# Context scores as split fp32r products in a one-core decoder layer, with the second batch's chain moved up in the tensor engine's queue

## The chip, the cores and the metric

The kernel runs on one core of one Trainium2 chip. The metric is the device time of one execution in microseconds; less is better. The profiled execution is one run of its own, so its time and its span are given apart from the median.

## The reference

One decoder layer: self-attention with a causal mask, attention over a context without projections, and a mixture of 16 experts with the best 4 per token, each behind a layer norm and added to its input. Two batches of 256 tokens, width 256, 16 heads of 16, 512 context tokens per batch.

```
x = x + attention(layernorm(x), Wq, bq, Wk, bk, Wv, bv, Wo, bo)      # 16 heads, causal

h = layernorm(x)
scores = einsum('bsd,bmd->bsm', h, ctx) / sqrt(256)
scores = where(mask[:, None, :], scores, -1e30)
x = x + (softmax(scores) @ ctx, or 0 for a batch whose mask is all false)

h = layernorm(x)
logits = h @ router_weight.T + router_bias
w = softmax of the 4 largest logits, at their experts, else 0
x = x + sum_e w[:, e] * (((clip(up_e, -7, 7) + 1) * glu(min(gate_e, 7))) @ down_e + down_bias_e)
```

## The kernel before

Five engines run one instruction stream each, written out by hand in the order in which each engine executes it. A semaphore count stands wherever one engine needs another's result. Nothing reorders the streams, so the place of a call in a block is its place in the queue.

**Tiles.** Tokens lie in four chunks of 128 (0 and 1 are batch 0, 2 and 3 are batch 1). `PS` is the accumulator memory, eight banks of 512 columns. `XH` and `XL` are the high and low part of the transposed activations in fp32r: an fp32 product is made there from three fp32r products (high by high, low by high, high by low). The experts have always been computed like that (`first_gate_up`, L1085, for expert 0, L1119 for the others, L1135 for the down projection). `WHg`, `WLg` are the split weights: the scalar engine writes the high part (L352), GpSimd the low part (L296).

**Self-attention.** A loop over `v` from 0 to 17, two steps a head group. In each the tensor engine does scores (L933, L937), transposes of the probabilities (L947) and, in odd steps, the product with V (L961). The vector engine adds the causal mask and takes the row maximum in one instruction (L668), the scalar engine exponentiates (L382), and both copy the transposed probabilities back (L693, L414). Batch 0 is done by step 10; its output projection and residual fill the later steps.

**Context attention.** For chunk `c`: `context_scores` (L984, fp32 product with `ctxT`, two matmuls, and a third that adds the mask penalty `pen` of one partition through `ones_bf`), `context_max` (L636) and `context_exp` (L386), `context_turn` (L992), `context_take` (L394), `context_values` (L998), `context_out` (L649). Chunks 0 and 1 begin when the loop ends. The second batch's self-attention output is turned back (L969), divided (L609, L610), turned again (L874), projected (L978) and added (L616) among them; then it is centred, turned and copied to `xT`, and chunks 2 and 3 follow. `rstds` (L282) on GpSimd takes the inverse roots for each of the norms.

**Router and first expert.** The last norm is turned and copied to `xT` (L435, L440), from there copied to `XH` (L445), and the rest goes to `XL` (L736). The router's logits are fp32 products with `xT` (`logits_of`, L1010). Some 17 small vector instructions (L750 to L773) choose the experts. `first_gate_up` does expert 0 batch by batch. `keep_warm` (L883) puts unneeded bf16 products in gaps.

**Mask.** The mask is loaded into one partition, cast (L589), and in step 5 made into `pen` and into the flag of a batch with any valid token (L683, L684), which one small matmul (L1033) spreads over the partitions.

Of the kernel before, what the change touches and what calls it, by code (L numbers as in the profile page):

```python
# [6 lines left out]
F32 = mybir.dt.float32  # L7
# [7 lines left out]
P = 128  # L15
B, S, D = 2, 256, 256
M = 512
# [25 lines left out]
def decoder_layer(nc, x_d, ctx_d, ctxT_d, wqkv_d, wo_d, params_d, rows_d, mask_d, dbias_d, we_d, out_d):  # L43
    ctx = ExitStack()
    with ctx:
# [9 lines left out]
        x = sb("x", [P, NC, D])  # L55
        ctx_sb = sb("ctx_sb", [P, B * KM, D])
        ctxT = sb("ctxT", [P, B * KD, M])
        wqkv = sb("wqkv", [P, 3, KD, D])
# [3 lines left out]
        mask8 = sb("mask8", [1, B * M], U8)  # L62
# [13 lines left out]
        ones_bf = sb("ones_bf", [1, P], BF16)  # L76
# [3 lines left out]
        one1 = sb("one1", [1, P])  # L80
# [23 lines left out]
        maskf = sb("maskf", [1, B * M])  # L104
        pen = sb("pen", [1, B * M], BF16)
        valid1 = sb("valid1", [1, B])
        valid = sb("valid", [P, B])
        xmax = sb("xmax", [P, NC])
# [42 lines left out]
        xpt = [keys_flat[:, (2 + i) * M:(3 + i) * M].rearrange("p (c q) -> p c q", q=P) for i in range(2)]  # L151

# [23 lines left out]
        pen_done, valid_ps, valid_done = sem("pen_done"), sem("valid_ps"), sem("valid_done")  # L176
# [70 lines left out]
        def _(pool):  # L247
# [24 lines left out]
            g.memset(ones_bf[:, :], 1.0)  # L272
            g.memset(ones_f[:, :], 1.0)
            g.memset(one1[:, :], 1.0)
# [35 lines left out]

            low_keys(0)
# [3 lines left out]
            low_gate_up(1, 1)  # L315
            for n in range(1, 5):
                rstds(n)
# [17 lines left out]
        def _(act):  # L335
# [5 lines left out]
            act.dma_start(mask8[:, :], mask_d.rearrange("(a n) -> a n", a=1)).then_inc(mask_in, 16)  # L341
# [44 lines left out]
            def context_exp(c):  # L386

                act.wait_ge(xbias_done, c + 1)
                if c >= 2:
                    act.wait_ge(xpT_done, c - 1)  # L390
                a.activation(xp[c % 2], PS[:, XS_BANK[c], :], ACT.Exp, bias=xbias[:, c:c + 1], scale=xscale[:, c:c + 1],
                             accum_out=xsum[:, c:c + 1]).then_inc(xexp_done, 1)

            def context_take(c):  # L394
                act.wait_ge(xpT_done, c + 1)
                if c >= 2:
                    act.wait_ge(xav_done, c - 1)
                a.activation(xpt[c % 2].rearrange("p h q -> p (h q)"), PS[:, XT_BANK[c], :], ACT.Copy
                             ).then_inc(xpt_done, 1)

            for v in range(NV + 2):
# [20 lines left out]
                if v == NV:  # L422
                    context_exp(0)
# [5 lines left out]
            context_take(0)  # L429
            context_exp(1)  # L430

            def take_turned(dst, b, bank, n, done):

                act.wait_ge(lnT_done, n)
                a.activation(dst[:, :, b * S:(b + 1) * S], PS[:, bank, :].rearrange("p (k n) -> p k n", k=KD), ACT.Copy  # L435
                             ).then_inc(done, 1)
# [6 lines left out]
            def high_x(b, count, tokens):  # L443
                act.wait_ge(xT_done[b], count)
                a.activation(XH[:, :, tokens], xT[:, :, tokens], ACT.Copy).then_inc(xh_done, 1)  # L445

            take_chunk(attT, 2, 7, 5, attT_done[1])
            context_take(1)
            take_chunk(attT, 3, 3, 6, attT_done[1])
            take_chunk(xT, 2, 7, 7, xT_done[1])  # L450
            take_chunk(xT, 3, 3, 8, xT_done[1])
            context_exp(2)
            take_turned(xT, 0, 0, 9, xT_done[0])
            context_exp(3)
            context_take(2)
            high_x(0, 3, slice(0, S))
            context_take(3)
            take_chunk(xT, 2, 6, 10, xT_done[1])
            high_x(1, 4, slice(S, S + P))
            take_chunk(xT, 3, 4, 11, xT_done[1])  # L460
            high_x(1, 5, slice(S + P, T))
# [65 lines left out]
        def _(dve):  # L527
# [61 lines left out]
            link(v_.tensor_copy(maskf[:, :], mask8[:, :]))  # L589
# [68 lines left out]

            for v in range(NV + 2):
# [13 lines left out]
                if v == NV:  # L673
                    dve.wait_ge(lnT_done, 4)
# [35 lines left out]
                if v >= NV:  # L710
                    context_max(v - NV)
# [502 lines left out]
```

## Time and profile before

| | us |
|---|---|
| median of 3 runs | 232.87 (232.74 to 234.01) |
| the profiled execution's own time | 232.66 |
| its span | 230.9 |
| around the span | 1.76 |

| engine | busy us | share of the span |
|---|---|---|
| tensor, matmuls | 222.6 | 96% |
| tensor, weight loads | 177.8 | 77% |
| vector | 179.4 | 78% |
| scalar | 130.1 | 56% |
| GpSimd | 75.2 | 33% |

A matmul's end is modelled, so the step from one start to the next tells what it costs, and its own duration tells only when its result can be used. The clock granted to the tensor engine is full in all 40 slices of the page. From 91.2 us on the program is the loop over experts; what the change touches lies before that.

### The profile page before, as it was taken

Reading aid. Unit: us, or ns where it says so; the run is one execution under the profiler, and the core shown is the slowest. Engines: PE = TensorE matmul, PEld = TensorE weight load, DVE = VectorE, ACT = ScalarE, POOL = GpSimd, SP = SyncE. Lnnn points to the kernel's source line nnn. Section 1 sums busy time; section 2 is a strip of 40 time slices with the busy share of each in tenths; the row PEclk is TensorE's granted clock in tenths of the full one; section 3 lists DMA queues with packets and bytes.
Section 4 is the critical chain, followed back from the end, with each engine's and each line's share of the span. In section 5 each row is a group of like instructions: output and inputs, shape, how many; then the busy total and the mean of one; then the engine's idle time right before and its main releaser. Section 6 shows DMA issues by size and latency. Waiting matters only on the chain.

```text
span 230.9 us, 4563 instructions
## 1 busy us (share of the span) xinstructions
PE 222.6 (96%) x1481; PEld 177.8 (77%) x1481; DVE 179.4 (78%) x431; ACT 130.1 (56%) x258; POOL 75.2 (33%) x65
## 2 busy tenths in 40 slices
PE   7999989998999999989999999999999999999995
PEld 2588767875485788778888888888888888888884
DVE  3779896969267458679889879879879879879775
ACT  2138999766341617384484384385385385375561
POOL 6621460001002010426426426425425435435222
PEclk9999999999999999999999999999999999999999
DMA  5991042000000000022422431331331330410002
GB/s 170 381 387 34 0 140 91 3 4 0 0 3 0 0 0 4 0 62 76 139 60 77 136 71 65 136 79 57 136 88 48 136 102 34 136 45 0 1 3 91
DMA packets 7856, 17.30 MB, mean 75 GB/s; under 512 B 913, under 2 KB 2978, under 8 KB 7714
## 3 DMA queue, kind: packets, MB, share of 16 engines
q1 hardware_dynamic: 7232, 16.52, 21.8%
q10 hardware_dynamic: 610, 0.60, 0.9%
q8 instruction: 8, 0.13, 0.2%
q14 instruction: 6, 0.05, 0.1%
HBM read 16.59 MB, written 0.52 MB: 74 GB/s over the span
## 4 chain that ended last, share of the span: by engine, by line
PE 79%; DVE 9%; ACT 6%; issue 3%; POOL 2%; POOLq 0%; DVEq 0%; ACTq 0%
PE PS L1119 34%; PE PS L1135 20%; PE PS L987 3%; ACT pr L382 3%; PE PS L1001 3%; PE PS L1085 3%; DVE masked L668 2%; PE PS L947 2%; PE PS L961 2%; PE PS L978 2%; PE PS L895 2%; PE PS L883 1%; DVE HL L798 1%; PE PS L1165 1%; DVE qpar L574 1%
## 5 line engine op out<-in xcount | busy, mean ns | idle before, releaser
L296 POOL TENSOR_TENSOR WLg<-raw_g,WHg 128x1024 fp32r<-128x1024 f32 x16 | 38.2, 2390 | 58.4 <-ACT WHg L352 58.4
L793 DVE SCALAR_TENSOR_TENSOR pt<-pt 128x512 f32<-128x512 f32 x30 | 49.4, 1646 | 4.2 <-DVE pt L789 2.2
L478 ACT ACTIVATE HH<-pt 128x512 fp32r<-128x512 f32 x30 | 18.9, 632 | 52.3 <-DVE pt L793 52.1
L1119 PE MATMUL PS<-XH,WHg 128*128 128x512 f32 x120 | 47.0, 392 | 0.0
L1119 PE MATMUL PS<-XL,WHg 128*128 128x512 f32 x120 | 46.9, 390 | 0.0
L1119 PE MATMUL PS<-XH,WLg 128*128 128x512 f32 x120 | 46.7, 389 | 0.0
L1135 PE MATMUL PS<-WHd,HH 128*128 128x256 f32 x120 | 35.3, 294 | 1.0 <-DVE HL L798 0.8
L1135 PE MATMUL PS<-WLd,HH 128*128 128x256 f32 x120 | 33.9, 282 | 0.0
L1135 PE MATMUL PS<-WHd,HL 128*128 128x256 f32 x120 | 33.9, 282 | 0.0
L303 POOL TENSOR_TENSOR WLd<-raw_w,WHd 128x512 fp32r<-128x512 f32 x16 | 20.7, 1296 | 32.9 <-ACT WHd L358 32.9
L798 DVE TENSOR_TENSOR HL<-pt,HH 128x512 fp32r<-128x512 f32 x30 | 22.2, 738 | 11.0 <-ACT HH L478 11.0
L382 ACT ACTIVATE pr<-masked,nmax 128x128 f32<-128x128 f32 x64 | 23.7, 443 | 7.2 <-DVE nmax L668 7.2
L1135 PEld LDWEIGHTS PS<-WHd,HH 128*128 128x128 f32 x120 | 22.9, 190 | 6.4 <-issue 4.8
L1119 PEld LDWEIGHTS PS<-XH,WLg 128*128 128x128 f32 x120 | 22.5, 188 | 4.8
L1119 PEld LDWEIGHTS PS<-XH,WHg 128*128 128x128 f32 x120 | 22.6, 188 | 4.5 <-issue 0.2
L1119 PEld LDWEIGHTS PS<-XL,WHg 128*128 128x128 f32 x120 | 22.6, 188 | 4.1
L782 DVE SCALAR_TENSOR_TENSOR x<-PS,score,x 128x256 f32<-128x256 f32 x56 | 24.2, 473 | 0.0
L1135 PEld LDWEIGHTS PS<-WHd,HL 128*128 128x128 f32 x120 | 22.9, 191 | 0.0
L1135 PEld LDWEIGHTS PS<-WLd,HH 128*128 128x128 f32 x120 | 22.9, 191 | 0.0
L668 DVE CUSTOM_DVE_ANT_0 masked<-PS,causal 128x128 f32<-128x128 f32 x64 | 18.9, 350 | 3.3 <-PE PS L937 3.2
L472 ACT ACTIVATE pt<-PS,bup 128x512 f32<-128x512 f32 x30 | 20.6, 686 | 0.0
L469 ACT ACTIVATE pt<-PS,params 128x512 f32<-128x512 f32 x30 | 20.4, 679 | 0.0
(154 smaller groups left out, 358.5 us busy)
## 6 DMA issues: line engine op xcount, KB each, us to landing
raw_g<-we_d SPq DMA_DIRECT2D x16, 512.0 KB, 4.0
raw_w<-we_d SPq DMA_DIRECT2D x16, 256.0 KB, 2.6
ctxT<-ctxT_d SPq DMA_DIRECT2D x1, 1024.0 KB, 10.1
ctx_sb<-ctx_d SPq DMA_DIRECT2D x1, 1024.0 KB, 12.3
wqkv<-wqkv_d SPq DMA_DIRECT2D x3, 256.0 KB, 6.1
out_d<-x SPq DMA_DIRECT2D x4, 128.0 KB, 1.7
rows<-rows_d ACTq DMA_DIRECT2D x1, 264.0 KB, 5.7
x<-x_d ACTq DMA_DIRECT2D x2, 128.0 KB, 2.8
```

The source lines that it names most:

```text
L296: g.tensor_tensor(WLg[slot][:, :, :, :].rearrange("p k g f -> p (k g f)"), raw_g[slot][:, :], WHg[slot][:, :, :, :].rearrange("p k g f -> ...
L303: g.tensor_tensor(WLd[slot][:, :, :].rearrange("p k d -> p (k d)"), raw_w[slot][:, :], WHd[slot][:, :, :].rearrange("p k d -> p (k d)").bi ...
L382: i = a.activation(pr[:, v % 2, j, cols], masked[:, v % 2, j, cols], ACT.Exp, bias=nmax[:, v % 2, j, qc:qc + 1], scale=-1.0)
L469: a.activation(glu[:, m, :], PS[:, 2 * m, :], ACT.Gelu_apprx_sigmoid, bias=gub[:, bass.ds(e, 1), 0, m]).then_inc(glu_done, 1)
L472: a.activation(upc[:, m, :], PS[:, 2 * m + 1, :], ACT.Identity, bias=bup1[:, bass.ds(e, 1), m]).then_inc(up_done, 1)
L478: a.activation(HH[slot][:, m, :], hid[:, m, :], ACT.Copy).then_inc(hh_done, 1)
L668: i = v_.tensor_tensor_reduce(out=masked[:, v % 2, j, cols], in0=PS[:, 2 * (v % 3) + j, cols], in1=causal[:, cols], scale=1.0, scalar=HUGE ...
L782: v_.scalar_tensor_tensor(out=acc[:, c, :], in0=PS[:, 4 + 2 * slot + c // 2, (c % 2) * D:(c % 2 + 1) * D], scalar=score[:, c, bass.ds(e, 1 ...
L793: v_.scalar_tensor_tensor(out=hid[:, m, :], in0=glu[:, m, :], scalar=GLU_MAX, in1=upc[:, m, :], op0=ALU.min, op1=ALU.mult).then_inc(hid_do ...
L798: v_.tensor_tensor(HL[slot][:, m, :], hid[:, m, :], HH[slot][:, m, :].bitcast(F32), ALU.subtract).then_inc(hl_done, 1)
L1119: i = t.matmul(PS[:, 2 * m + part, :], w[slot][:, k, part, m * P:(m + 1) * P], xx[:, k, :], start=(n == 0), stop=(n == 3 * KD - 1))
L1135: i = t.matmul(PS[:, 4 + 2 * slot + c // 2, (c % 2) * D:(c % 2 + 1) * D], hh[slot][:, k, c * P:(c + 1) * P], w[slot][:, k, :], start=(n == ...
```

## The change

- `ctxT` is split into `keys_high0`, `keys_high1` and `keys_low` by four GpSimd instructions on 128x1024 (`split_keys`), the router's weights into `rth`, `rtl` (`split_router`). The new tiles lie over `x`, `ctxT` and `wqkv`.
- `context_scores` is six fp32r matmuls of 512 columns per chunk instead of two fp32 ones and one for the mask. `logits_of` is six fp32r matmuls of 16 columns per chunk instead of two fp32 ones.
- The mask is loaded into all 128 partitions. The vector engine reduces it to `valid`; GpSimd casts it and makes `pen` of it (`masks`). The matmul L1033 is gone. `context_max` adds `pen` and takes the maximum in one instruction whose sums go to SBUF (`xp`), and `context_exp` reads them there.
- The turned activations go from `PS` into `XH` (scalar engine) and as difference into `XL` (vector engine) without `xT` between.
- In the queues of all engines the second batch's turning back, turning and projection stand ahead of the context products of the first, the two halves of batch 0's `first_gate_up` stand around the last turn, batch 1's logits behind it, and the four `keep_warm` calls there are gone.

```diff
-        mask8 = sb("mask8", [1, B * M], U8)
+        mask8 = sb("mask8", [P, B * M], U8)
...
+            def masks():
...
+                pool.wait_ge(mask_in, 16)
+                linked(g.tensor_copy(pen[:, :], mask8[:, :]))
+                pool.wait_ge(valid_done, 1)
+                for b in range(B):
+                    g.tensor_scalar(pen[:, b * M:(b + 1) * M], pen[:, b * M:(b + 1) * M], valid[:, b:b + 1], -NEG,
+                                    ALU.subtract, ALU.mult).then_inc(pen_done, 1)
+            def split_router():
+                pool.wait_ge(param_in, 16)
+                g.tensor_copy(rth[:, :, :], routerT).then_inc(router_high, 1)
+                pool.wait_ge(router_high, 1)
+                g.tensor_tensor(rtl[:, :, :], routerT, rth[:, :, :].bitcast(F32), ALU.subtract).then_inc(router_low, 1)
+            def split_keys(b):
+                pool.wait_ge(ctxT_in, 16)
+                if b == 1:
+                    pool.wait_ge(v_ps, NC)
+                raw = ctxT[:, b * KD:(b + 1) * KD, :]
+                g.tensor_copy(cth[b], raw).then_inc(cth_done, 1)
+                pool.wait_ge(cth_done, b + 1)
+                g.tensor_tensor(ctl[b], raw, cth[b].bitcast(F32), ALU.subtract).then_inc(ctl_done, 1)
...
             low_gate_up(1, 1)
+            masks()
+            split_router()
+            split_keys(0)
+            split_keys(1)
             for n in range(1, 5):
                 rstds(n)
...
-                if v == NV:
-                    context_exp(0)
+                if v == NV - 1:
+                    high_tokens(7, 4, slice(0, S), yh_done)
...
-            link(v_.tensor_copy(maskf[:, :], mask8[:, :]))
+            v_.tensor_reduce(valid[:, :], mask8[:, :].rearrange("p (b m) -> p b m", b=B), AX.X, ALU.max).then_inc(valid_done, 1)
...
-                link(v_.tensor_reduce(xmax[:, c:c + 1], PS[:, XS_BANK[c], :], AX.X, ALU.max))
+                link(v_.tensor_tensor_reduce(out=xp[c % 2], in0=PS[:, XS_BANK[c], :], in1=pen[:, c // QC * M:(c // QC + 1) * M],
+                                             scale=1.0, scalar=-HUGE, op0=ALU.add, op1=ALU.max, accum_out=xmax[:, c:c + 1]))
...
                 if v == NV:
-                    dve.wait_ge(lnT_done, 4)
-                    v_.tensor_copy(xT[:, :, 0:S], PS[:, 7, :].rearrange("p (k n) -> p k n", k=KD)).then_inc(xT_done[0], 1)
+                    low_tokens(7, yh_done, 1, slice(0, S), yl_done)
...
-            normalise(x3, 3, (0, 1))
             context_max(2)
             context_max(3)
+            normalise(x3, 3, (0, 1))
...
-                pe.wait_ge(xT_done[b], 2 if b == 0 else c - QC + 2)
+                pe.wait_ge(yl_done, 1 if b == 0 else c)
+                pe.wait_ge(ctl_done, b + 1)
...
-                t.matmul(PS[:, XS_BANK[c], :], ones_bf[:, :], pen[:, b * M:(b + 1) * M], start=False, stop=True
-                         ).then_inc(xs_done, 1)
+                    for xx, w in ((XH, cth), (XL, cth), (XH, ctl)):
+                        i = t.matmul(PS[:, XS_BANK[c], :], xx[:, k, c * P:(c + 1) * P], w[b][:, k, :],
+                                     start=(n == 0), stop=(n == 3 * KD - 1))
```

The tensor engine's queue behind the self-attention loop, before: context scores, turning back (L969), context values, turns of `att` (L874), projection (L978).

```order
L987 MATMUL PS<-ctxT,xT 128x512 x2
L988 MATMUL PS<-pen,ones_bf 128x512
L995 MATMUL PS<-ident,qpar 128x128 x4
L969 MATMUL PS<-ident,osum 128x128 x8
L1001 MATMUL PS<-ctx_sb,qpar 128x256 x4
L874 MATMUL PS<-ident,att 128x128 x2
L995 MATMUL PS<-ident,qpar 128x128 x4
L874 MATMUL PS<-ident,att 128x128 x2
L978 MATMUL PS<-wo,attT 128x256 x4
L1001 MATMUL PS<-ctx_sb,qpar 128x256 x4
```

The same place after (L1039 is the context turn, L1009 the turning back, L1045 the context values, L1018 the projection).

```order
L1030 MATMUL PS<-keys_low,XH 128x512
L1009 MATMUL PS<-ident,osum 128x128 x8
L1039 MATMUL PS<-ident,qpar 128x128 x4
L914 MATMUL PS<-ident,att 128x128 x4
L1018 MATMUL PS<-wo,attT 128x256 x4
L1045 MATMUL PS<-ctx_sb,qpar 128x256 x4
L1039 MATMUL PS<-ident,qpar 128x128 x4
L914 MATMUL PS<-ident,xn 128x128 x4
L1045 MATMUL PS<-ctx_sb,qpar 128x256 x4
L1030 MATMUL PS<-keys_high,XH 128x512
```

The projection no longer stands behind `context_values(0)` and `context_turn(1)`, and `context_values(1)` has moved behind the turns of batch 1's centred rows, straight ahead of its scores.

The scalar engine's queue at the end of the self-attention loop, before.

```order
L414 ACTIVATE pt<-PS 128x384
L421 ACTIVATE osum<-PS 128x256
L414 ACTIVATE pt<-PS 128x384
L391 ACTIVATE qpar,xsum<-PS,xbias,xscale 128x512
L421 ACTIVATE osum<-PS 128x256
```

The same place after.

```order
L463 ACTIVATE pt<-PS 128x384
L470 ACTIVATE osum<-PS 128x256
L448 ACTIVATE XH<-PS 128x2x256
L463 ACTIVATE pt<-PS 128x384
L470 ACTIVATE osum<-PS 128x256
L430 ACTIVATE qpar,xsum<-qpar,xbias,xscale 128x512
```

The high part of batch 0's turned rows is a new step of this queue, behind the copies of step 15; in front of the scores stood one copy on the vector engine before.

GpSimd's queue between the attention's weight splits and the second `rstds`, after; before, nothing stood between the rows L302 and L288.

```order
L302 TENSOR_TENSOR WLg<-raw_g,WHg 128x1024
L325 CAST pen<-mask 128x1024
L328 TENSOR_SCALAR pen<-pen,valid 128x512 x2
L334 CAST rth<-params 128x32
L336 TENSOR_TENSOR rtl<-params,rth 128x32
L344 CAST keys_high<-ctxT 128x1024
L346 TENSOR_TENSOR keys_low<-ctxT,keys_high 128x1024
L344 CAST keys_high<-ctxT 128x1024
L346 TENSOR_TENSOR keys_low<-ctxT,keys_high 128x1024
L288 TENSOR_TENSOR rstd<-ve,half 128x2 x4
```

## Rows read from the trace of the kernel before

**Rows 1.** Stretch by engine: length, busy (instructions) PE, PEld, DVE, ACT, POOL, clock, DMA

```profile
57.69:91.22 33.53, 33.06 (x196) 23.54 (x195) 19.23 (x72) 12.66 (x29) 2.12 (x3) 1.00 0.00 0
100.13:217.00 116.87, 116.64 (x659) 99.90 (x660) 100.07 (x142) 68.95 (x111) 48.98 (x27) 1.00 0.26 83
```

**Rows 2.** Timeline of the tensor engine, context attention: start, us, instruction

```profile
57.69 1.96 PE L987 MATMUL PS<-ctxT,xT 128*128 128x512 f32 x4
...
59.89 0.86 PE L961 MATMUL PS<-pt,vp 128*32 128x128 f32 x24
...
63.40 1.04 PE L969 MATMUL PS<-ident,osum 128*128 128x128 f32 x8
...
67.02 2.04 PE L978 MATMUL PS<-wo,attT 128*128 128x256 f32 x8
...
71.91 1.98 PE L987 MATMUL PS<-ctxT,xT 128*128 128x512 f32 x4
...
76.87 0.60 PE L995 MATMUL PS<-ident,qpar 128*128 128x128 f32 x4
...
79.10 3.62 PE L1001 MATMUL PS<-ctx_sb,qpar 128*128 128x256 f32 x16
```

**Rows 3.** Timelines of the scalar and vector engine around the scores and splits

```profile
57.88 0.49 ACT L414 ACTIVATE pt<-PS 128x384 f32<-128x384 f32 x1
...
77.07 0.60 ACT L435 ACTIVATE xT<-PS 128x512 f32<-128x512 f32 x1 [0.63 <-PE PS L867]
...
79.53 0.69 DVE L736 TENSOR_TENSOR XL<-xT,XH 128x512 fp32r<-128x512 f32 x1 [0.65 <-ACT XH L445]
```

**Rows 4.** Chain that ended last: fp32r products of 256 and of 512 columns

```profile
82.72 2.86 PE PS L1085 x24
...
91.22 3.01 PE PS L1119 x12
```

**Rows 5.** Timeline of the tensor engine, the router's logits of one chunk

```profile
86.38 0.62 PE L1010 MATMUL PS<-params,xT 128*128 128x16 f32 x4
86.85 0.38 PE L883 MATMUL PS<-warm 128*128 128x512 bf16 x1
```

**Rows 6.** Timeline of the vector engine: row maximum, last norm, routing

```profile
74.60 0.68 DVE L639 TENSOR_REDUCE xmax<-PS 128x1 f32<-128x512 f32 x1
...
85.00 0.73 DVE L553 TENSOR_SCALAR xn<-x,mv,rstd 128x256 f32<-128x256 f32 x2 [0.81 <-POOL rstd L282]
...
87.87 0.21 DVE L750 TENSOR_TENSOR logits<-PS,rows 128x64 f32<-128x64 f32 x1
```

**Rows 7.** Timeline of GpSimd: fill, weight splits, inverse roots

```profile
3.93 0.94 POOL L276 MEMSET vp<- 128x1024 f32 x1
...
29.41 1.39 POOL L303 TENSOR_TENSOR WLd<-raw_w,WHd 128x512 fp32r<-128x512 f32 x1 [0.58 <-ACT WHd L358]
32.38 2.37 POOL L296 TENSOR_TENSOR WLg<-raw_g,WHg 128x1024 fp32r<-128x1024 f32 x1 [1.58 <-ACT WHg L352]
54.72 0.75 POOL L282 TENSOR_TENSOR rstd<-ve,half 128x2 f32<-128x2 f32 x1 [19.97 <-DVE ve L626]
```

**Rows 8.** Timeline of the vector engine around the mask, at the start and in step 5

```profile
10.35 0.67 DVE L589 CAST maskf<-mask 1x1024 f32<-1x1024 uint8 x1
...
12.61 1.53 DVE L574 TENSOR_SCALAR qpar<-PS,params,parity 128x512 f32<-128x512 f32 x2 [0.81 <-PE PS L895]
...
29.58 1.20 DVE L684 TENSOR_REDUCE valid<-maskf 1x2 f32<-1x1024 f32 x1
```

**Rows 9.** Timelines from the routing to expert 0's down projection, engine by engine

```profile
90.39 0.69 ACT L469 ACTIVATE pt<-PS,params 128x512 f32<-128x512 f32 x1
...
94.61 2.40 POOL L296 TENSOR_TENSOR WLg<-raw_g,WHg 128x1024 fp32r<-128x1024 f32 x1 [9.64 <-ACT WHg L352]
...
95.31 2.24 DVE L798 TENSOR_TENSOR HL<-pt,HH 128x512 fp32r<-128x512 f32 x1
...
100.13 0.39 PE L1135 MATMUL PS<-WHd,HH 128*128 128x256 f32 x1 [0.81 <-DVE HL L798]
```

More of the change, by code:

```diff
@@ L399, in context_take, with turned, high_tokens @@
                              ).then_inc(xpt_done, 1)
+            def turned(bank, tokens):
+                n = tokens.stop - tokens.start
+                return PS[:, bank, 0:KD * n].rearrange("p (k n) -> p k n", k=KD)
+            def high_tokens(bank, n, tokens, done):
+                act.wait_ge(lnT_done, n)
+                a.activation(XH[:, :, tokens], turned(bank, tokens), ACT.Copy).then_inc(done, 1)
             for v in range(NV + 2):
@@ L428, in _ @@
                     high_gate_up(1, 1, 0)
[L429 to L436, printed above, removed]
+            context_exp(0)
             def take_chunk(dst, c, bank, n, done):
@@ L657, in context_stats, with low_tokens @@
                 row_stats(x3, c)
+            def low_tokens(bank, high, n, tokens, done):
+                dve.wait_ge(high, n)
+                count = tokens.stop - tokens.start
+                v_.tensor_tensor(XL[:, :, tokens], PS[:, bank, 0:KD * count].rearrange("p (k n) -> p k n", k=KD),
+                                 XH[:, :, tokens].bitcast(F32), ALU.subtract).then_inc(done, 1)
             for v in range(NV + 2):
@@ L709, in _ @@
                     centre(0)
-                if v >= NV:
-                    context_max(v - NV)
+                if v == NV + 1:
+                    dve.wait_ge(pen_done, B)
+                    context_max(0)
             for qc in range(QC):
                 outputs(1, qc, (5, 0)[qc])
-            dve.wait_ge(valid_done, 1)
+            context_max(1)
             context_weight(0)
-            context_weight(1)
-            context_out(0)
-            for j in range(QC):
-                residual(1, j, PS[:, (6, 5)[j], 0:D])
+            residual(1, 0, PS[:, 6, 0:D])
+            residual(1, 1, PS[:, 5, 0:D])
             centre(1)
             context_scale(1)
+            context_out(0)
+            context_weight(1)
+            low_tokens(7, yh_done, 2, slice(S, S + P), yl_done)
+            low_tokens(3, yh_done, 3, slice(S + P, T), yl_done)
             context_out(1)
@@ L1003, in context_values, with logits_of @@
                 i.then_inc(xav_done, 1)
-            def logits_of(b, count, chunks):
-                pe.wait_ge(xT_done[b], count)
+            def logits_of(count, chunks):
+                pe.wait_ge(router_low, 1)
+                pe.wait_ge(xl_done, count)
                 for c in chunks:
+                    n = 0
                     for k in range(KD):
-                        i = t.matmul(PS[:, 7, c * E:(c + 1) * E], xT[:, k, c * P:(c + 1) * P], routerT[:, k, :],
-                                     start=(k == 0), stop=(k == KD - 1))
+                        for xx, w in ((XH, rth), (XL, rth), (XH, rtl)):
+                            i = t.matmul(PS[:, 7, c * E:(c + 1) * E], xx[:, k, c * P:(c + 1) * P], w[:, k, :],
+                                         start=(n == 0), stop=(n == 3 * KD - 1))
+                            n += 1
                 i.then_inc(logit_ps, 1)
@@ L1094, in _ @@
                 turn_chunk(xn, QC + j, (6, 4)[j])
[L1095 to L1100 removed]
+            first_gate_up(0, 1)
+            logits_of(2, (2,))
+            logits_of(3, (3,))
+            first_gate_up(1, 0)
+            first_gate_up(1, 1)
             def turn_scores():
```

142 lines of the change are left out of this document (65 added, 77 removed).

## The prediction, made before the changed kernel was run

> **What bounds the kernel now.** I read the busy time by stretch first. Between the first context scores at 57.69 us and expert 1 at 91.22 the tensor engine is busy 33.06 of 33.53 us, and from 100.13 to 217 it is busy 116.64 of 116.87 [rows 1]. So behind 100.13 the end moves by as much as the product at 100.13 moves, and that is the date to follow. Next come the waits. The product at 100.13 waited 0.81 us for the vector engine's `HL` [rows 9]. The first `HL` of expert 0, at 95.31, lasted 2.24 us [rows 9], where the `XL` of the same shape lasts 0.69 [rows 3]; GpSimd's `WLg` ran from 94.61 to 97.01 [rows 9], and `HL` ended half a microsecond behind it. That `WLg` hangs, through the scalar engine's copies and the first product of expert 0, on the routing, whose first instruction stands at 87.87 [rows 6]. So two dates count: when the router's logits are there, and when the tensor engine gets to expert 1.
>
> The Trainium skill (SBUF — State Buffer, "Who interferes with whom") says that a vector instruction with two SBUF inputs and a GpSimd instruction that reads SBUF exclude each other for a whole instruction. By that rule the 2.24 us are a wait for `WLg`, and the trace agrees.
>
> **The scores.** Before, one chunk's scores took the tensor engine 2.20 us (57.69 to 59.89, [rows 2]). After, it is six fp32r products of 512 columns. Twelve such took 3.01 us with the tail of the last [rows 4], some 0.235 each, so six take 1.4. That saves 0.8 a chunk, 3.2 us of tensor time in four. I do not take that as the gain, because each place has a wait of its own, so I walk the queues with these durations.
>
> **First scores.** Before, they stood ready behind the last attention turn, at 57.69. After, the scalar engine must write `XH`, and its queue is free for that at 57.88, where the next copy of step 15 began. The copy takes 0.60 and the difference 0.69 [rows 3], with two handovers of some 0.05. The scores start at about 59.25, 1.55 later, and end at 60.65, 0.75 later. Behind this wait stand, on the tensor engine, the last product with V and, on the vector engine, the copy of the last probabilities that this product needs; both come within the 0.75. The second scores win 0.8 back: the tensor engine is level with before at about 62.85.
>
> **Second batch's chain.** The turning back (8 transposes, 1.04 us, [rows 2]) comes ahead of one context turn (4 transposes, so 0.5): 0.5 earlier. The projection stood at 67.02, behind one chunk's context values (two chunks take 3.62, [rows 2]; I take 1.75 a chunk) and another context turn. Both now come behind it. It starts at 65.1, as soon as the two `att` chunks are divided, turned and copied, and is 1.9 earlier; so are batch 1's centred rows. But `context_values(1)` now stands between them and the scores of chunk 2, which begin at 71.8 against 71.91 [rows 2]. Two scores take 2.8 for 4.4: 1.7 won at their end.
>
> **Maxima.** Adding the mask inside the maximum costs little: the old maximum takes 0.68 [rows 6], the new one has the same 512 columns and a read of the result behind it. I take 0.77. But the vector engine reaches chunk 2 only behind `context_out(1)`, statistics and variances, at 73.6; the old one stood at 74.60 [rows 6]. With exponent and handovers the context turn of chunk 2 starts at 75.6 against 76.87 [rows 2]: 1.25 won. Two turns, the transposes and two times 1.75 of values bring the end of the values to 81.2, 1.35 earlier. The last norm hangs on it and comes at 83.65 against 85.00 [rows 6].
>
> **Router and expert 0.** Here the win is spent. The fp32 logits of a chunk take 0.47 for four passes of 16 columns, 0.117 each (86.38 to 86.85, [rows 5]), as long as a product of 256 columns (24 in 2.86, 0.119, [rows 4]): something other than the columns bounds them. The same pitch for fp32r makes 12 products 1.4 us (0.91 before) and each six 0.69 (0.47 before). The tensor engine goes on almost without a gap: logits of batch 0 to 82.6, half of expert 0 (12 products, 1.43) to 84.05, two turns to 84.6, the other half to 86.05, six logits to 86.75, six to 87.45. The splits of the last rows (scalar from 84.3, vector to 85.8) hide behind the second half. The last product is usable 0.2 later, and the same walk on the kernel before comes out 0.15 early, so the routing starts at 87.8 against 87.87 [rows 6]: 0.1 won of 1.35. The half of `first_gate_up` ahead of the last logits, and 0.9 us of extra logits, ate it. Batch 1's 24 products end at 90.5.
>
> **To the loop.** Expert 1 started at 91.22 [rows 4]. It needs the tensor engine (90.5) and a bank that the scalar engine has emptied, at 91.08 before [rows 9], which hangs on the routing: 0.1 earlier. `WLg` and the blocked `HL` hang on the same routing: the product at 100.13 comes 0.1 earlier, with a longer wait before it.
>
> **GpSimd.** The new work starts where the last `WLg` ends, at 34.75 (32.38 plus 2.37, [rows 7]). No row shows a cast there. From above: five instructions of 1024 at 2.37, two of 512 at 1.39, two small at 0.75, 16.1 us, to 50.9. From below: three of 1024 at the fill's 0.94, two at 2.37, two of 512 at 0.47, 8.5 us, to 43.3 [rows 7]. It is needed at 54.72 by the `rstd` behind it [rows 7] and later by the scores. I take it as hidden, 3.8 us clear even at the upper end. The attention's vector instructions in that stretch read `PS` and at most one SBUF tile, unlike the blocked `HL`, so I charge no contention. If that cover were gone, every microsecond past 54.72 would count whole.
>
> The Trainium skill (GPSIMD Engine Reference, "Engine selection") puts one-input work on GpSimd near line rate. By that the list would end near my lower end; nothing in the sum changes.
>
> **Start.** The mask is 128 KB for 1 KB. The reduction takes 1.20 where the cast took 0.67 at 10.35; the next need is at 12.61, for which the vector engine had waited 0.81 [rows 8]. The 0.53 fits in it. It costs nothing if the mask has landed by 10.6; between 0 and 0.3 us, I take 0. The mask work that leaves step 5 (1.20 of it in [rows 8]) was no gain either: the scalar engine set the pace there.
>
> **Sum.** Start 0, scores and chains -1.35, logits and the half expert +1.25: -0.1 us. The profiled execution of 232.66 would be 232.56; it lies 0.21 under the median of 232.87. Forecast: 232.8.
>
> **Rivals.** A measurement of this kernel can tell about 0.5% from no change, 1.16 us.
> 1. The win reaches the routing. If an fp32r product with 16 columns costs half that pass (the lower bound is the 0.036 of the products with V, 24 in 0.86, [rows 2]), 0.6 more comes early. If then `HL` also slips in ahead of `WLg`, the wait of 0.81 goes: -0.1 -0.6 -0.8 = -1.5, 231.4. For it: what bounds a pass may be less in fp32r. Against it: `WLg` began 0.7 ahead of `HL`, and both move together. Chance of all this, or of as much through a shorter chain of norms, 0.25; of the first half alone (232.2) 0.12.
> 2. GpSimd becomes late. From 20.0 us of new work on (54.72 less 34.75) each further microsecond delays batch 0's scale, the exponents and the chain by one. The inverse root takes 0.75 for two columns [rows 7], so this engine has slow operations, and one with two steps and a scalar from memory is not in the trace. With 22 us: +2.0, 234.9. Chance 0.07.
> 3. The mask lands late, one for one from 10.6 on; at 11.5 +0.9, 233.7. Chance 0.06, half of it beyond the 0.5%.
> 4. The clock. It is full in both stretches [rows 1]. The warming calls go, and gaps of 1.4 and 1 us come in. If it fell to 1.2 GHz for 2.5 us worth of products, +2.5: 235.3. Chance 0.03.
>
> The forecast itself has 0.47; its own spread is 232.2 to 233.3, mostly the pitch of the small products (0.14 for 0.117 gives +0.4). Faster by over 0.5%: 0.25. Within: 0.62. Slower: 0.13. The range reaches down to rival 1, 231.4, and to 233.9, past rival 3.
>
> **What would show it.** Right: the first key product at 59.2; the projection near 65.1; the last context values done near 81.2; logits for the vector engine at 87.8; again a first `HL` of over 2 us; a wait of about a microsecond near 100. Wrong: small products at half the pitch; a first `HL` of 0.69; GpSimd busy at 54; a clock below full.

## The result

The kernel went from 232.74 us (median of 5 runs, 232.55 to 234.01) to 230.81 (median of 5, 230.67 to 232.31), a ratio of 0.9924 with a 95% interval of 0.9896 to 0.9952. That is 1.9 us faster, outside the predicted range, where the forecast had said 232.8 and no measurable change.

In some executions, of every kernel here, TensorE is granted half its clock in some stretch, and the mean granted clock of the run reads 0.99 in place of 1.00. The kernel before takes 232.5 to 232.9 us with and without it in most executions (a few lie between 233.1 and 233.8), and 233.9 to 234.2 where the mean reads 0.985. The changed kernel takes 230.7 to 231.0 without it (231.4 once) and 232.2 to 232.7 with it. A few runs are longer still, such as two of ten of the changed kernel, run again, at 235.2 and 235.4 with a mean of 0.98, and no ratio here uses them. The profiled execution of the changed kernel (232.31, span 230.2) is one with a stretch of half clock.

Two stretches of that execution follow, in the columns of [rows 1]. The first is the first context scores; the second is as long as the second line of [rows 1] and starts at the same product:

```profile
59.84:62.30 2.46, 2.46 (x6) 1.81 (x6) 0.41 (x1) 0.00 (x0) 0.00 (x0) 0.50 0.00 0
...
101.93:218.80 116.87, 116.81 (x671) 102.91 (x672) 97.52 (x144) 72.53 (x114) 55.73 (x28) 1.00 0.26 83
```

The second line is what the prediction did not expect. The tensor engine is as busy as before, 116.81 of 116.87 us, and yet 671 matmuls are recorded where [rows 1] had 659 in the same time. Its busy share had hidden a wait. The product that the prediction followed came later, not earlier: 101.93 against 100.13 [rows 9]. From it to the end of the span it was 130.8 us before (230.9 less 100.13) and is 128.3 now (230.2 less 101.93). So the change lost 1.8 us ahead of the loop over the experts in this execution, and the loop, whose code did not change, gave back 2.5.

Where the 1.8 went is in the timelines of the changed kernel (start, us, instruction, in brackets the idle time before it and what ended it): the vector engine at the start, the tensor engine's first attention score and first context score, its projection, and then GpSimd, the vector and the tensor engine around expert 0:

```profile
11.61 1.22 DVE L628 TENSOR_REDUCE valid<-mask 128x2 f32<-128x1024 uint8 x1 [1.56 <-DMA mask<-mask_d]
...
16.56 0.45 PE L973 MATMUL PS<-kT,qpar 32*128 32x128 f32 x3 [0.72 <-DVE HL L619]
...
59.84 0.79 PE L1030 MATMUL PS<-keys_high,XH 128*128 128x512 f32 x1 [1.30 <-DVE XL L705]
60.43 0.63 PE L1030 MATMUL PS<-keys_high,XL 128*128 128x512 f32 x1
60.85 0.63 PE L1030 MATMUL PS<-keys_low,XH 128*128 128x512 f32 x1
...
67.30 1.99 PE L1018 MATMUL PS<-wo,attT 128*128 128x256 f32 x8
...
96.41 2.40 POOL L302 TENSOR_TENSOR WLg<-raw_g,WHg 128x1024 fp32r<-128x1024 f32 x1 [10.72 <-ACT WHg L393]
...
97.12 2.24 DVE L838 TENSOR_TENSOR HL<-pt,HH 128x512 fp32r<-128x512 f32 x1
...
101.93 0.38 PE L1174 MATMUL PS<-WHd,HH 128*128 128x256 f32 x1 [0.81 <-DVE HL L838]
```

The mask landed at about 11.6, and with it the first attention score moved from 15.96 to 16.56 (the work behind it by 0.7). The six context products, at half clock in this execution, come every 0.43 us in place of the 0.235 of [rows 4]: 1.2 us. The rest, 1.8 less 0.7 less 1.2, is -0.1, which is what the prediction had for the whole context stage.

One kernel of the experiments (`after_dve_pause`, the changed kernel with one tiny instruction more) was profiled with a mean clock of 0.999, and there the changed stage can be read without any half clock. Its first attention score is at 16.55 us, 0.6 later than before. Then come the last norm, the routing and the product that the prediction followed:

```profile
84.39 0.73 DVE L593 TENSOR_SCALAR xn<-x,mv,rstd 128x256 f32<-128x256 f32 x2 [0.81 <-POOL rstd L289]
...
88.33 0.22 DVE L791 TENSOR_TENSOR logits<-PS,rows 128x64 f32<-128x64 f32 x1 [1.77 <-PE PS L1060]
...
100.60 0.39 PE L1177 MATMUL PS<-WHd,HH 128*128 128x256 f32 x1 [0.81 <-DVE HL L841]
```

So with a full clock the product comes 0.5 us later than the 100.13 of [rows 9]: 0.6 from the start, -0.1 from the context stage.

### The profile page after: what moved, and what is told of

It is laid out like the page before. It is cut to its first block, busy times and chain, and to the rows that moved or that the text cites. A ratio compares the mean times of both kernels' runs of the same rounds, so it can differ in the third digit from the quotient of the medians.

```text
span 230.2 us, 4585 instructions
## 1 busy us (share of the span) xinstructions
PE 217.4 (94%) x1484; PEld 181.1 (79%) x1485; DVE 173.5 (75%) x434; ACT 131.2 (57%) x256; POOL 92.3 (40%) x72
## 4 chain that ended last, share of the span: by engine, by line
PE 74%; DVE 10%; ACT 6%; DMA 4%; issue 3%; ACTq 1%; DVEq 0%
PE PS L1158 35%; PE PS L1174 19%; DMA mask<-mask_d 4%; PE PS L1030 3%; PE PS L1045 3%; ACT pr L423 3%; DVE masked L717 2%; PE PS L987 2%; PE PS L1001 2%; PE PS L1018 2%; PE PS L1125 1%; PE PS L1204 1%; DVE HL L838 1%; PE PS L973 1%; PE PS L1057 1%
## 5 line engine op out<-in xcount | busy, mean ns | idle before, releaser
L302 POOL TENSOR_TENSOR WLg<-raw_g,WHg 128x1024 fp32r<-128x1024 f32 x16 | 41.2, 2574 | 61.0 <-ACT WHg L393 61.0
L838 DVE TENSOR_TENSOR HL<-pt,HH 128x512 fp32r<-128x512 f32 x30 | 30.7, 1025 | 12.2 <-ACT HH L517 12.2
L833 DVE SCALAR_TENSOR_TENSOR pt<-pt 128x512 f32<-128x512 f32 x30 | 36.2, 1206 | 4.2 <-DVE pt L829 1.8
L1174 PE MATMUL PS<-WHd,HH 128*128 128x256 f32 x120 | 34.2, 285 | 0.9 <-DVE HL L838 0.8
L309 POOL TENSOR_TENSOR WLd<-raw_w,WHd 128x512 fp32r<-128x512 f32 x16 | 23.4, 1463 | 22.0 <-ACT WHd L399 22.0
## 6 DMA issues: line engine op xcount, KB each, us to landing
ctxT<-ctxT_d SPq DMA_DIRECT2D x1, 1024.0 KB, 11.6
```

The source lines that it names most:

```text
L302: g.tensor_tensor(WLg[slot][:, :, :, :].rearrange("p k g f -> p (k g f)"), raw_g[slot][:, :], WHg[slot][:, :, :, :].rearrange("p k g f -> ...
L309: g.tensor_tensor(WLd[slot][:, :, :].rearrange("p k d -> p (k d)"), raw_w[slot][:, :], WHd[slot][:, :, :].rearrange("p k d -> p (k d)").bi ...
L833: v_.scalar_tensor_tensor(out=hid[:, m, :], in0=glu[:, m, :], scalar=GLU_MAX, in1=upc[:, m, :], op0=ALU.min, op1=ALU.mult).then_inc(hid_do ...
L838: v_.tensor_tensor(HL[slot][:, m, :], hid[:, m, :], HH[slot][:, m, :].bitcast(F32), ALU.subtract).then_inc(hl_done, 1)
L1174: i = t.matmul(PS[:, 4 + 2 * slot + c // 2, (c % 2) * D:(c % 2 + 1) * D], hh[slot][:, k, c * P:(c + 1) * P], w[slot][:, k, :], start=(n == ...
```

## What happened in the loop

The loop over the experts has two bodies, one for each of two buffers, and a pass does two experts. In the kernel before, GpSimd's `WLg` and the vector engine's second activation product (`pt<-pt`, the step that makes `hid`) start within 0.05 us of each other in every expert of it (0.12 in the one ahead of it), and the one that starts later is held: a race. Both hang on the scalar engine's copy `HH`: the one through the next copy `WHg`, the other through `HL` and the clamp. The kernel before, one such place, engine by engine:

```profile
171.05 0.63 ACT L478 ACTIVATE HH<-pt 128x512 fp32r<-128x512 f32 x1 [0.35 <-DVE pt L793]
171.59 1.05 ACT L352 ACTIVATE WHg<-raw_g 128x1024 fp32r<-128x1024 f32 x1
...
171.72 0.69 DVE L798 TENSOR_TENSOR HL<-pt,HH 128x512 fp32r<-128x512 f32 x1 [0.70 <-ACT HH L478]
172.33 0.42 DVE L789 TENSOR_SCALAR pt<-pt 128x512 f32<-128x512 f32 x1
172.84 2.89 DVE L793 SCALAR_TENSOR_TENSOR pt<-pt 128x512 f32<-128x512 f32 x1
...
172.80 2.39 POOL L296 TENSOR_TENSOR WLg<-raw_g,WHg 128x1024 fp32r<-128x1024 f32 x1 [2.95 <-ACT WHg L352]
```

The same place after, in the second body of the loop:

```profile
172.10 0.69 DVE L833 SCALAR_TENSOR_TENSOR pt<-pt 128x512 f32<-128x512 f32 x1
172.71 0.87 DVE L822 SCALAR_TENSOR_TENSOR x<-PS,score,x 128x256 f32<-128x256 f32 x2
173.50 2.12 DVE L838 TENSOR_TENSOR HL<-pt,HH 128x512 fp32r<-128x512 f32 x1
...
172.14 2.93 POOL L302 TENSOR_TENSOR WLg<-raw_g,WHg 128x1024 fp32r<-128x1024 f32 x1 [3.04 <-ACT WHg L393]
```

Before, `WLg` is 0.04 us ahead, and the product is held until it is done: 2.89 us for work of 0.69. After, the product is 0.04 ahead; now `WLg` is held (2.93 for 2.39) and then `HL` (2.12 for 0.69). The Trainium skill (SBUF — State Buffer, "Who interferes with whom") says that issue order and not the shape of the operation decides who blocks; these two places agree, and they show how narrow the decision is.

It matters who is held, because the second product stands on the ring that feeds the tensor engine (product, `HH`, `WHd`, bank reading, product), and `HL` only on the down projection. The scalar engine's groups between 127 and 210 us, before and then after (count | busy, mean ns | idle before it, and what ended most of it):

```profile
L472 ACT ACTIVATE pt<-PS,bup 128x512 f32<-128x512 f32 x19 | 13.0, 687 | 0.0
L469 ACT ACTIVATE pt<-PS,params 128x512 f32<-128x512 f32 x19 | 12.9, 678 | 0.0
L478 ACT ACTIVATE HH<-pt 128x512 fp32r<-128x512 f32 x19 | 12.0, 632 | 32.2 <-DVE pt L793 32.2
```

```profile
L508 ACT ACTIVATE pt<-PS,params 128x512 f32<-128x512 f32 x21 | 14.3, 680 | 3.5 <-PE PS L1158 3.5
L511 ACT ACTIVATE pt<-PS,bup 128x512 f32<-128x512 f32 x20 | 13.7, 686 | 5.6 <-PE PS L1158 5.2
L517 ACT ACTIVATE HH<-pt 128x512 fp32r<-128x512 f32 x20 | 12.6, 632 | 22.4 <-DVE pt L833 21.4 <-PE PS L1174 0.7
```

Before, the scalar engine never waits for the tensor engine's products: the ring of scalar and vector engine set the pace, and two experts took 17.15 us (`WLg` at 172.80, the next of that body at 189.95). After, it waits 8.7 us for them: two experts take 16.66 (172.14, 188.80) and the tensor engine is the bound. Experiment 1 bears this out: with the short product in both bodies the pace stays at 16.68. In the page the mean of all thirty such products fell from 1646 to 1206 ns and that of `HL` rose from 738 to 1025.

In the changed kernel this begins at the second body's first pass, and there GpSimd starts late:

```profile
114.59 2.40 POOL L302 TENSOR_TENSOR WLg<-raw_g,WHg 128x1024 fp32r<-128x1024 f32 x1 [3.08 <-ACT WHg L393]
118.89 1.30 POOL L309 TENSOR_TENSOR WLd<-raw_w,WHd 128x512 fp32r<-128x512 f32 x1 [1.90 <-ACT WHd L399]
123.50 2.65 POOL L302 TENSOR_TENSOR WLg<-raw_g,WHg 128x1024 fp32r<-128x1024 f32 x1 [3.31 <-ACT WHg L393]
```

From the end of the scalar copy to the start of `WLg` it is 0.17 us at 114.59, 0.53 at 123.50, and 0.25 in every later pass of this body (0.17 still in the first body). The 0.08 between 0.17 and 0.25 is just what flips the order, from `WLg` 0.04 us ahead to the product 0.04 ahead. The experiments ask where this comes from and what it is worth.

## Experiments

Each is named by what it starts from. "Full clock" means the runs with a mean granted clock of 1.00.

**1. Does losing the race cost what the loop lost? `before_pool_pause`.** In the kernel before, a tiny operation ahead of each `WLg` of the loop:

```
+                if not isinstance(e, int):
+                    g.tensor_tensor(pause[:, bass.ds(e, 1), :], half[:, :].unsqueeze(1), half[:, :].unsqueeze(1), ALU.subtract)
                 g.tensor_tensor(WLg...
```

> The kernel before with one small GpSimd instruction (128x4) ahead of each WLg of the loop, so that WLg starts 0.2 to 0.3 us later and the vector engine's second product stands first. Phase theory: that product lasts 0.69 us, WLg is held instead, an expert takes 8.34 us for 8.6, in 11 or 12 experts 2.3 to 3.0 us less: 229.8 to 230.5. Rival (the loop gained through something static of the changed kernel, such as where its tiles or its code lie): the time stays at 232.7 or rises by up to 0.3.

229.61 and 229.71 at full clock, 230.93 to 231.06 at 0.993 and 232.38 at 0.985, beside 232.71: ratio 0.9915 (0.9882 to 0.9948). Both bodies now have the short product:

```profile
162.60 0.69 DVE L796 SCALAR_TENSOR_TENSOR pt<-pt 128x512 f32<-128x512 f32 x1
163.21 0.87 DVE L785 SCALAR_TENSOR_TENSOR x<-PS,score,x 128x256 f32<-128x256 f32 x2
164.00 2.27 DVE L801 TENSOR_TENSOR HL<-pt,HH 128x512 fp32r<-128x512 f32 x1
...
163.31 2.41 POOL L299 TENSOR_TENSOR WLg<-raw_g,WHg 128x1024 fp32r<-128x1024 f32 x1
```

So the order in this race is enough for the loop's gain, and it is worth 3 us to the kernel before, with no part of the change. That kernel is also faster than the changed one. `before_again`, the kernel before unchanged on the same chip, gave 232.63 with the product at 2.9 us in every expert of the loop.

> The kernel before, traced a second time. Phase theory: in the loop over experts GpSimd's WLg again starts 0.03 to 0.05 us ahead of the vector engine's second product in every expert, that product lasts 2.9 us in every expert, and an expert takes 8.6 us. Chance theory (who starts first is drawn anew in each execution): some of the products of 0.69 us, experts of 8.34 us between.

**2. The other way round: `after_dve_pause`.** A fill on the vector engine ahead of the second product, to hand the race back.

```
                     wait(dve, hl_done, e * 2 + (m - 1))
+                    if not isinstance(e, int) and m == 1:
+                        v_.memset(pause[:, :], 0.0)
```

> The changed kernel with one small vector instruction ahead of the second product of each expert of the loop, so that GpSimd's WLg stands first by 0.05 to 0.1 us in every expert. Phase theory: the product lasts 2.9 us in all of them, an expert takes 8.6 us or a little more, and the gain of the loop goes: 2.2 to 3 us more than the changed kernel, 233.0 to 233.8. Rival (static): 230.8 to 231.0.

The expected 233.0 to 233.8 did not come, and the run decides nothing: 230.68 (clock 0.999) and 230.99 (1.00), 231.54 to 232.16 at 0.993. The fill moved the product by only 0.03 us, and in the second body it still went first, in a tie of the records (both at 170.87, product 0.69, `WLg` 2.95). So the race was not handed back; the recorded starts are a little coarser than what decides.

**3. The start: `after_valid_late`.** The mask reduction moves from the start into step 5 of the attention.

```
-            dve.wait_ge(mask_in, 16)
-            v_.tensor_reduce(valid[:, :], mask8[:, :]...)
...
+                if v == 5:
+                    dve.wait_ge(mask_in, 16)
+                    v_.tensor_reduce(valid[:, :], mask8[:, :]...)
```

> The changed kernel with the reduction of the mask moved from the start into step 5 of the self-attention, so that nothing at the start waits for the mask's load. If the late mask cost the start its 0.7 us: 230.1 (230.0 to 230.3), and the first attention scores at 15.9 us for 16.56. Rival (the start was late for another reason, such as the other loads landing about a microsecond later): 230.8, scores as late as now. Either holds only if the loop keeps its 8.34 us.

229.94, 230.06 and 230.25 at full clock against 230.67 to 231.0 of the changed kernel: 0.7 us. In its trace the first attention score stands at 15.71, where the kernel before has 15.96. So the late mask was the whole loss at the start.

**4. Where the loop lies: `before_pool_pad` and `after_pool_pad`.** The change puts nine instructions into GpSimd's stream ahead of the loop and takes two fills out; the loop itself is untouched. Here seven tiny subtractions, where GpSimd is idle:

```
+            for n in range(7):
+                g.tensor_tensor(pad[:, n, :], half[:, :], half[:, :], ALU.subtract)
             for n in range(1, 5):
                 rstds(n)
```

> The kernel before with seven tiny GpSimd subtractions (128x4, about 0.1 us each) put behind its low weight parts and ahead of the expert loop, where GpSimd is idle in both kernels. They take no shared resource at any moment of the loop; all they change is where the loop's instructions lie in GpSimd's stream, by as many instructions as the change adds net. Placement theory: the weight subtraction of the loop's second body then starts about 0.25 us after its ScalarE copy (0.16 before) with one late start near 120 us, the second activation product of those experts takes 0.7 us in place of 2.9, and the time falls by 2.2 to 2.6 us to 230.1 to 230.6. Rival (the changed context stage itself sets the phase of the loop): nothing moves, 232.7, product 2.9 us in every expert.

> The changed kernel with the same seven tiny GpSimd subtractions ahead of its loop, which moves the loop on by seven more instructions. Placement theory: the pattern of long and short second products can move to the other body or vanish; if it vanishes (2.9 us in every expert) the time is 233.0 to 233.4, if it stays 230.7 to 231.0. Rival (the context stage sets it): the pattern and 230.8 stay whatever the placement. A time above 232.5 with products of 2.9 us would show placement alone; 230.8 with the pattern as it was leaves it open.

`before_pool_pad` came out wrong for both theories: 233.52 at full clock, median 233.68, ratio 1.0038 (1.0024 to 1.0052), every second product at 2.9 us. But its trace kept the placement theory alive: the late start is there, but one GpSimd operation further on, on `WLd` of the second body:

```profile
121.73 2.40 POOL L297 TENSOR_TENSOR WLg<-raw_g,WHg 128x1024 fp32r<-128x1024 f32 x1 [2.95 <-ACT WHg L355]
126.38 1.29 POOL L304 TENSOR_TENSOR WLd<-raw_w,WHd 128x512 fp32r<-128x512 f32 x1 [2.25 <-ACT WHd L361]
```

That is 0.51 us behind its copy, later passes 0.25. There it wins no race and costs: two experts take 17.26 us (`WLg` at 148.02 and at 165.28). `after_pool_pad` lost the late start and the pattern altogether: 234.0 in the profiled run, median 235.29, ratio 1.0119 (1.0098 to 1.014), slower than the kernel before and above the 233.4 expected at most.

**5. Put it where the change puts it: `before_pool_pad9` and `before_pool_pad15`.** In the instruction streams, `WLg` of the second body is two instructions ahead of the `WLd` that was late with seven; so nine should place it. (The change's own count is nine too: seven net, and two of its new instructions wait for two things, taken as one more each, a reading made after seven had missed.) The first body's is six further ahead: fifteen.

> The kernel before with nine tiny GpSimd subtractions ahead of the loop. With seven, the late instruction of the loop was the down-weight subtraction of the second body (0.51 us after its ScalarE copy once, 0.25 from then on, 0.16 elsewhere), two instructions of GpSimd's stream behind the gate/up-weight subtraction of that body, which is the late one in the changed kernel (0.53, then 0.25). Placement theory: two more move the late start onto that gate/up-weight subtraction; then the second product of the second body takes 0.7 us from the third or fourth expert on, as in the changed kernel, and the untouched context stage runs at 230.0 to 230.6. Rival (a late start of GpSimd alone does not flip who goes first, something of the changed stage does): the late start is there, but every product stays at 2.9 us, and the time is 232.7 to 233.7.

> The same with fifteen. Placement theory: the late start falls on the gate/up-weight subtraction of the first body, and there the short product follows it; 230.0 to 230.6 again. Rival: 232.7 to 233.7, or the gain stays with the second body whatever the placement.

Both came within some 0.3 us of what the theory said. Nine: 230.0, 230.52 and 230.78 at full clock, median of ten 231.08, ratio 0.9932 (0.9906 to 0.9957). Fifteen: 229.69, 229.76 and 229.94, ratio 0.9882 (0.984 to 0.9925). The first late starts, nine and then fifteen:

```profile
121.64 2.66 POOL L297 TENSOR_TENSOR WLg<-raw_g,WHg 128x1024 fp32r<-128x1024 f32 x1 [3.31 <-ACT WHg L355]
```

```profile
113.30 2.64 POOL L297 TENSOR_TENSOR WLg<-raw_g,WHg 128x1024 fp32r<-128x1024 f32 x1 [3.44 <-PE PS L1122]
```

With nine, the second body from then on, the vector engine and GpSimd, as in the changed kernel:

```profile
171.19 0.69 DVE L796 SCALAR_TENSOR_TENSOR pt<-pt 128x512 f32<-128x512 f32 x1
171.80 0.87 DVE L785 SCALAR_TENSOR_TENSOR x<-PS,score,x 128x256 f32<-128x256 f32 x2
172.59 2.11 DVE L801 TENSOR_TENSOR HL<-pt,HH 128x512 fp32r<-128x512 f32 x1
...
171.23 2.92 POOL L297 TENSOR_TENSOR WLg<-raw_g,WHg 128x1024 fp32r<-128x1024 f32 x1 [3.04 <-ACT WHg L355]
```

With fifteen, the first body has the short products and the second the long ones. The untouched context stage with nine idle instructions gives what the change gave.

The DMA queues tell more of the late start. Between 120 and 125 us, with nine, a queue of kind "instruction" (q14) moves one packet, as it does in the changed kernel; in the kernel before it moves none there:

```profile
q1 hardware_dynamic: 256, 0.72, 45.5%
q14 instruction: 1, 0.01, 0.7%
```

With fifteen that packet falls between 110 and 115, with seven between 125 and 130: each time the stretch of the first late start. So the late spot goes with a fetch of instructions. It did not wait for this packet, though: the packet starts 0.6 to 0.9 us after the late instruction did (124.13 and 123.50 in the changed kernel, 122.48 and 121.64 with nine, 114.15 and 113.30 with fifteen, 127.00 and 126.38 with seven). Other packets of this queue, such as one at 100.05 in the kernel before, have no late GpSimd instruction beside them. The Trainium skill (Advanced Engine Details and Errata, "ISA Cache") gives an engine two cache lines of 256 instructions. A loop that lies across the edge between two such lines would meet it at one spot in every pass, and one late spot agrees with that; the packet here is 0.01 MB, smaller than the page's line of 16 KB. What the late instruction waits for, 0.35 us the first time and 0.08 in each later pass, no row shows.

**6. One instruction: `after_pool_pad6` and `after_pool_pad7_b`.** By the same count the changed kernel, which has nine already, needs six to put the late start on the first body's `WLg`. The second kernel is `after_pool_pad` once more.

> The changed kernel with six tiny GpSimd subtractions ahead of its loop. With none the late start is on the gate/up-weight subtraction of the second body, with seven it was on nothing that matters. Counted by the kernels with seven, nine and fifteen, six put it on the gate/up-weight subtraction of the first body. Placement theory: short second products in the first body from its first pass on (near 115 us), and 230.0 to 230.6 with TensorE at full clock, up to 1.5 us more with a fall of the clock. Rival (any padding of the changed kernel makes it slow, as seven did): 234 or more.

> The changed kernel with seven again, one more tiny subtraction than the kernel beside it. No late start on a gate/up-weight subtraction, every second product 2.9 us, 233.5 to 235.8 as before; so one instruction of 0.1 us ahead of the loop is worth 3 us or more. Rival: its 235.3 was chance of those runs, and it comes near 232.7.

Six: 230.16 to 230.63 at full clock, median of ten 231.71. Seven: 234.13 at full clock, median of seven 235.68, ratio 1.0092 (1.0055 to 1.0128). One subtraction of 128x4, hidden, moves the kernel by 3.5 to 4.0 us at full clock. The two places, six and then seven:

```profile
114.85 2.65 POOL L303 TENSOR_TENSOR WLg<-raw_g,WHg 128x1024 fp32r<-128x1024 f32 x1 [3.44 <-PE PS L1161]
```

```profile
115.96 2.41 POOL L303 TENSOR_TENSOR WLg<-raw_g,WHg 128x1024 fp32r<-128x1024 f32 x1 [3.08 <-ACT WHg L396]
```

With seven the packet starts at 110.23 us in the trace of `after_pool_pad`, ahead of the loop's first `WLg` at 113.43, and no `WLg` or `WLd` of the loop starts late.

Seven is also the change without the luck of the loop: 234.13 at full clock, 1.4 us slower than the kernel before. In the profile of `after_pool_pad` the clock was full up to the loop, and the walk can be read undisturbed (first attention score, expert 0's down projection):

```profile
16.62 0.45 PE L976 MATMUL PS<-kT,qpar 32*128 32x128 f32 x3 [0.83 <-DVE HL L622]
...
100.79 0.39 PE L1177 MATMUL PS<-WHd,HH 128*128 128x256 f32 x1 [0.81 <-DVE HL L841]
```

**7. The context stage alone: `after_late_pause` and `after_late_pause_warm`.** The changed kernel with experiments 1 and 3 together; the second with `keep_warm(2, 5)` ahead of the first context scores.

> The changed kernel with the mask reduction moved off the start and the small GpSimd pause ahead of each weight subtraction in the loop. Against the kernel before with the pause alone (229.66 with TensorE at full clock) only the changed context stage is left, its start repaired: my walk gives -0.15, so 229.5. If the context change is worth 1 us or more, 228.7 or less; if it costs, over 229.8.

> The same with five idle products of 128x512 on a free bank ahead of the first context scores, where TensorE stands 1.3 us for the vector engine's low tokens. They fill that stand and nothing waits for them, so at full clock 229.5 again. If the stand is what brings the fall of the clock in that stage (granted clock 0.992 in the profiled run of the changed kernel, 1.3 us), no run shows it any more and the median falls by up to 1 us below that of the kernel without them; else some runs still show 0.992 and some 1.3 us more.

229.85 and 229.91 at full clock, where 229.5 was expected, against 229.61 and 229.71 of `before_pool_pause` (on another chip), which differs by the change with its start repaired. So with the race set the same way in both, the change makes the kernel 0.2 us slower. The spans are 227.7 and 227.8 against 227.9 and 228.0, so inside the span the change wins 0.2 us; outside it loses 0.4. Time less span is 2.1 to 2.2 us in the kernels with the changed stage, 1.7 to 1.8 in those without, and 1.9 in `after_dve_pause`, which has the changed stage too; so the stage alone does not set it, and what it is no row shows.

The warming calls took nothing off the times: three of four runs at 0.993, 231.1 to 231.3, and 230.11 at full clock. In the one trace the half clock lies between 100 and 106 us instead of at the scores. Whether the calls moved it is not shown, since the unchanged `after_again` has it between 102 and 106 as well; what brings it stays open. `after_again` gave 230.65 to 230.93 in three of four runs at full clock (231.42 in the fourth) and 232.24 to 232.68 at 0.993.

> The changed kernel once more, unchanged. Late start and short products in the second body of the loop as before, median 230.7 to 231.0 with TensorE at full clock, some runs 1.3 to 1.5 us more with a fall of the clock to half in some stretch of the context stage or later.

## Why the prediction was wrong, step by step

- **"So behind 100.13 the end moves by as much as the product at 100.13 moves": this step failed,** and with it the forecast. It rested on the 116.64 busy of 116.87 us. The busy time of back-to-back matmuls is modelled up to the next one and swallowed a wait of 0.24 us an expert (17.15 against 16.66 for two). The product at 100.13 came later, by 0.5 us at full clock and by 1.8 in the profiled run, and the end came 1.9 us earlier. The rows that would have told were there: the scalar engine waiting for nothing of the tensor engine in the loop, and the second product at 2.9 us in every expert. The prediction read the blocked `HL` of expert 0 in [rows 9], priced it, and did not ask the same of the loop.
- **The order of the moved code.** GpSimd's new work was charged by its time alone and came out at nothing. It also moves the loop along in its stream, and by that the order of the race flips in the second body: -2.6 us, more than the whole -1.9. That the new instructions put the late start just there was luck: two instructions fewer put it on `WLd`, and that cost 0.8 us (`before_pool_pad`).
- **Start, sized wrong.** The mask was taken to land by 10.6; it landed at 11.6, and rival 3, priced at 0.9 for 11.5, came true at 0.7 (experiment 3).
- **Context stage, right.** In the trace of `after_dve_pause`, with the start's 0.6 us taken off: first scores at 59.14 (forecast 59.25), projection 65.3 (65.1), last norm 83.8 (83.65), routing 87.7 (87.8). The forecast was -0.1 in all; measured -0.1 there, -0.2 in experiment 7 and 0.0 in `after_pool_pad` (16.62 and 100.79 above, both 0.66 later than before).
- **Small products, right.** The six fp32r products of 16 columns of a chunk come at a pitch of 0.112 us against 0.117 assumed, so rival 1's condition did not hold; the routing they feed started at 89.66:

```profile
88.59 0.26 PE L1057 MATMUL PS<-rth,XL 128*128 128x16 f32 x1
88.70 0.26 PE L1057 MATMUL PS<-rtl,XH 128*128 128x16 f32 x1
88.81 0.26 PE L1057 MATMUL PS<-rth,XH 128*128 128x16 f32 x1
...
89.66 0.23 DVE L790 TENSOR_TENSOR logits<-PS,rows 128x64 f32<-128x64 f32 x1 [1.77 <-PE PS L1057]
```

- **GpSimd, hidden as forecast,** with one term out of its bounds. The list ran from 35.37 to 48.09, inside 43.3 to 50.9, but the two-step operation took 2.05 us for 512 columns where I had 1.39 at most, and the cast of 1024 took 1.04:

```profile
35.37 1.04 POOL L325 CAST pen<-mask 128x1024 f32<-128x1024 uint8 x1
36.50 4.09 POOL L328 TENSOR_SCALAR pen<-pen,valid 128x512 f32<-128x512 f32 x2
```

- **The clock.** Rival 4 came in the profiled run, in the very gap it named, at half the price (1.2 us). Inside the loop the kernel before has such stretches too, and there they cost nothing (98 to 104 us in the trace of `before_again`, 232.63). Where the tensor engine bounds the loop they cost: 230.96 for 229.66 in `before_pool_pause`, with the stretch at 100 to 104. The place at the first context scores is new: five of the nine traces with the changed stage have a stretch between 58 and 66 us, none of the six without. Why is open.
- **Outside the span, not foreseen.** +0.4 us, cause open.
- **The account at full clock:** ahead of the loop +0.5 (start +0.6, context -0.1), outside the span +0.4, loop -2.6 (from the product to the end 128.2 us for 130.8): -1.7. Measured: 232.7 to 230.8, -1.9; the 0.2 between the two is no more than runs of one kernel differ by. Had the race not flipped, the change would have cost 1.4 us (`after_pool_pad7_b`).

## What to carry to other kernels

A busy share near one is no proof of a bound: look in the loop for engines that wait for the supposed bottleneck, and where none does, as here before the change, doubt it. Where two instructions that exclude each other start within 0.1 us of each other in every pass, the kernel can have two speeds, and anything that moves code or a handover by a few hundredths of a microsecond can switch them; set that order on purpose (here one small operation, 3 us) before judging any other change. A gain of a change must be tried with the loop's luck held fixed, or it is credited to the wrong lines.

## What the runs showed of the hardware that I had not expected

- Where a fetch of instructions falls into the GpSimd loop, one instruction starts 0.35 us late once, 0.6 to 0.9 us ahead of the fetched packet, and 0.08 to 0.09 late in each later pass. Two, six and seven instructions more ahead of the loop moved or removed the spot.
- A vector instruction that starts 0.04 us behind GpSimd's waits for all of it (2.9 us for 0.69); one that starts 0.04 ahead takes 0.69 and makes GpSimd's 0.54 longer.
- A copy of 128 KB that spreads a 1 KB mask over 128 partitions took 8.9 us from issue to landing beside the weight loads. Much of that is the queue: the 16 KB of `dbias` on it took 8.7, and 6.1 in the kernel before.
